# A cross-attention block: the up-projection by one level of Strassen's product

## The reference, cut to what matters

```
q = layer_norm(query, ln1_g, ln1_b)
qh = (q @ wq + bq); kh = (context @ wk + bk); vh = (context @ wv + bv)    # split into 16 heads
scores = einsum(qh, kh) / sqrt(32), causal over positions
x = query + (softmax(scores) applied to vh) @ wo + bo
h = layer_norm(x, ln2_g, ln2_b)
return x + gelu(h @ w1 + b1) @ w2 + b2          # exact GELU; w1 is 512 x 2048, w2 is 2048 x 512
```

## Time and profile before

| | us |
|---|---|
| runs (two) | 1866.86 and 1867.20, median 1867.03 |
| span of the profiled execution | 1864.5 |
| span of slots 0 and 1 | 253.8 |
| one steady slot | 108.9 |
| slot 16 | 86.5 |
| TensorE, VectorE, ScalarE, POOL busy | 1799.3, 1247.9, 640.5, 443.8 |

### The profile page before, as it was taken

How to read it: one execution, slowest core, us unless ns; L and a number is a source line. 1 busy time by engine, 2 the same in 40 slices (tenths; PEclk the granted TensorE clock), 3 DMA queues, 4 the chain that set the end, 5 groups by cost and what they waited for, 6 DMA issues and landing times.

```text
span 1864.5 us, 26584 instructions
## 1 busy us (share of the span) xinstructions
PE 1799.3 (97%) x10213; PEld 819.6 (44%) x10213; DVE 1247.9 (67%) x1930; ACT 640.5 (34%) x799; POOL 443.8 (24%) x376
## 2 busy tenths in 40 slices
PE   6678899999999999999999999999999999999999
PEld 3233344444444444444444444444444444444444
DVE  6767757667675767757676676757677576866622
ACT  5654424242232424223242422324242232424211
POOL 2523114131320314122141313203141221413200
PEclk8878999999999999999999999999999999999999
DMA  8230232314123241412323131332413133231200
GB/s 288 54 105 12 46 91 46 91 23 79 35 60 77 46 91 23 78 36 57 80 46 91 19 81 38 57 80 46 91 21 77 40 57 79 46 91 19 50 23 23
DMA packets 287738, 116.27 MB, mean 62 GB/s; under 512 B 262616, under 2 KB 264192, under 8 KB 287616
## 3 DMA queue, kind: packets, MB, share of 16 engines
q1 hardware_dynamic: 287616, 114.61, 27.4%
HBM read 31.22 MB, written 16.78 MB: 26 GB/s over the span
## 4 chain that ended last, share of the span: by engine, by line
PE 90%; DVE 5%; POOL 1%; ACT 1%; DMA 1%; issue 1%; SPq 0%; DVEq 0%; ACTq 0%
PE ff_ps L1141 34%; PE ff_ps L1384 34%; PE at_ps L1141 18%; PE at_ps L1298 2%; PE at_ps L1318 1%; DVE w_all L829 1%; POOL arena L560 1%; DVE arena L829 0%; DVE xhat L818 0%; DMA arena<-in_L_xattn_wk 0%; PE ff_ps L1213 0%; DVE arena L1114 0%; DVE arena L1061 0%; PE at_ps L1213 0%; DVE smax L1059 0%
## 5 line engine op out<-in xcount | busy, mean ns | idle before, releaser
L1141 PE MATMUL ff_ps<-arena,w_all 128*128 128x512 f16 x3072 | 701.8, 381 | 2.3 <-DVE arena L829 2.3
L1384 PE MATMUL ff_ps<-w_all,arena 128*128 128x512 f16 x3072 | 698.0, 379 | 0.9 <-DVE arena L829 0.9
L1141 PEld LDWEIGHTS ff_ps<-arena,w_all 128*128 128x128 f16 x3072 | 300.4, 98 | 371.7 <-issue 15.6
L1384 PEld LDWEIGHTS ff_ps<-w_all,arena 128*128 128x128 f16 x3072 | 294.4, 98 | 358.6 <-issue 6.4
L753 ACT ACTIVATE arena<-ff_ps,b1p,scales 128x512 f32<-128x512 f32 x256 | 198.5, 775 | 634.6 <-PE ff_ps L1141 634.3
L1114 DVE TENSOR_SCALAR arena<-arena,scales 128x512 f16<-128x512 f32 x256 | 150.1, 586 | 215.6 <-ACT arena L753 215.5
L829 DVE SCALAR_TENSOR_TENSOR arena<-arena,scales 128x512 f16<-128x512 f32 x256 | 239.2, 934 | 9.1
L511 POOL TENSOR_TENSOR rstd<-ve,minus_half 128x1 f32<-128x1 f32 x128 | 85.6, 669 | 561.1 <-DVE ve L801 561.1
L555 POOL TENSOR_TENSOR x_sb<-x_sb,bo_row 128x512 f32<-128x512 f32 x64 | 92.6, 1477 | 359.8 <-PE at_ps L1298 350.5
L687 ACT ACTIVATE norm_hl<-xhat 128x512 f16<-128x512 f32 x120 | 73.9, 628 | 287.6 <-DVE xhat L818 287.6
L560 POOL TENSOR_TENSOR arena<-arena,rsum 128x1024 f32<-128x1024 f32 x64 | 124.8, 1971 | 176.1 <-DVE rsum L1087 176.1
(11 more groups left out here) (154 smaller groups left out, 1377.3 us busy)
## 6 DMA issues: line engine op xcount, KB each, us to landing
...
```

The lines of the kernel that those rows point to most:

```text
L1141: last = nc.tensor.matmul(out_ap, s, m, start=(i == 0), stop=(i == n - 1))
L1384: last = nc.tensor.matmul(ff2_ps[:, t, :], pair[:, s, rows], m[:, j], start=(j == 0 and i == 0), stop=(j == NJ - 1 and i == 2))
```

## The change

FF1 is done in pairs of groups. For pair q the 256 hidden rows are two blocks of 128, the 512 pieces of the contraction two halves of 256, and the 512 tokens two halves of 256 columns. One level of Strassen's product in Winograd's form makes the four result quarters C11, C12, C21, C22 from seven block products instead of eight. The block sums of the weights (S1 to S4) are made once, when W1 is converted; those of the activations (T1 to T4) once per chunk, by `block_sums_of` (step K) on VectorE, so the second norm leaves seven blocks instead of four, each with its two halves (`blocks_low` and ScalarE's step D). The sums U, V and the quarters C are made on VectorE from the products in PSUM, the first product being copied to SBUF by ScalarE first. GELU then reads SBUF; its high half moves from VectorE to ScalarE.

To make room, `hT` has one buffer of seven blocks instead of two of four, keys and values of all batches lie in DRAM and are loaded per batch by ten DMAs, and the first norm's steps A and C of the next chunk move from the end of a slot to groups 1 and 2 of the next (`PLAN_NORM`, step a and c). The second norm's transposes become two of 128 x 2048, two of 128 x 1024 and two of 128 x 512.

```diff
-    25: [("O", 0), ("O", 1), ("G", 0), ("O", 2), ("G", 1), ("D", 0), ("O", 3), ("G", 2), ("D", 1),
-         ("G", 3), ("D", 2), ("D", 3)],
-    27: [("N", 0), ("N", 1), ("N", 2), ("N", 3)],
-    29: [("A", 0), ("A", 1), ("C", 0), ("A", 2)], 30: [("C", 1), ("A", 3), ("C", 2)], 31: [("C", 3)],
+    25: [("O", 0), ("O", 1), ("G", 0), ("O", 2), ("G", 1), ("K", 0), ("O", 3)],
+    26: [("D", 0), ("G", 2), ("G", 3), ("K", 1)], 27: [("N", 0), ("D", 1), ("N", 1)],
+    28: [("N", 2), ("N", 3)],
...
+PLAN_NORM = {
+    2: [("a", 0), ("a", 1), ("c", 0)], 3: [("a", 2), ("c", 1)], 4: [("a", 3), ("c", 2)], 5: [("c", 3)],
+}
...
+            def move_blocks(n, blocks, done):
+
+                sp.sem_inc(moves_begun, 1)
+                sp.dma_start_transpose(hT[:, blocks, :, :, n * P:(n + 1) * P].rearrange("p b a k n -> p (b a k) n"),
+                                       norm_blocks[n][:, blocks].rearrange("p b a n -> p (b a n)")).then_inc(done[n], 16)
...
+                    for n in range(2):
+                        sp.wait_ge(blocks_lo, 2 * c + (n + 1))
+                        sp.sem_inc(moves_begun, 1)
+                        wait(sp, first_p26, NPAIRS * c)
+                        move_blocks(n, slice(B11, T2 + 1), h_first)
+                    for n in range(2):
+                        wait(sp, second_p4, NPAIRS * c)
+                        for blocks in (slice(T1, T4 + 1), slice(B22, B22 + 1)):
+                            move_blocks(n, blocks, h_second)
...
-                        nc.scalar.activation(gelu_full[g % 2], ff1_ps[:, g % 2, :], ACT.Gelu,
-                                             bias=b1p[:, g:g + 1], scale=col(C1)).then_inc(g_full, 1)
+                    if ff and g < NJ and g % 2 == 0:
+                        q = g // 2
+                        act.wait_ge(first_p17, NPAIRS * c + (q + 1 - NPAIRS))
+                        nc.scalar.activation(quarters[:, COPY], ff1_ps[:, 0, 0:HF], ACT.Copy).then_inc(p1_moved, 1)
+                    elif ff and g < NJ:
+                        q = g // 2
+                        for j, done in ((2 * q, c12_set), (2 * q + 1, c21_set)):
+                            half = ff_in[:, j % 2 * CHUNK:(j % 2 + 1) * CHUNK]
+                            act.wait_ge(done, NPAIRS * c + (q + 1 - NPAIRS))
+                            nc.scalar.activation(half, half, ACT.Gelu, bias=b1p[:, j:j + 1], scale=col(C1)
+                                                 ).then_inc(g_full, 1)
+                            act.wait_ge(g_full, NJ * c + (j + 1 - NJ))
+                            nc.scalar.activation(g_pair[j % NG][:, 0, :], half, ACT.Copy, scale=col(SG)
+                                                 ).then_inc(g_hi, 1)
...
+            def block_sums_of(c, n):
...
+                nc.vector.tensor_tensor(t3_t1, y1.to_broadcast([P, 2, HF]), norm_f32[:, 1:3], ALU.subtract
+                                        ).then_inc(block_sums, 1)
+                dve.wait_ge(block_sums, begun + 1)
+                nc.vector.tensor_tensor(t2, y2, t1, ALU.subtract).then_inc(block_sums, 1)
+                dve.wait_ge(block_sums, begun + 2)
+                nc.vector.tensor_tensor(t4, x2, t2, ALU.subtract).then_inc(block_sums, 1)
...
+                    if ff and g < NJ and g % 2 == 0:
+
+
+                        dve.wait_ge(first_p26, NPAIRS * c + (q + 1 - NPAIRS))
+                        dve.wait_ge(p1_moved, NPAIRS * c + (q + 1 - NPAIRS))
+                        wait(dve, g_lo, NJ * c + (2 * q - NJ))
+                        nc.vector.tensor_tensor(quarters[:, C11:U + 1:4], ff1_ps[:, 1, :].rearrange("p (b n) -> p b n", b=2),
+                                                quarters[:, COPY:COPY + 1].to_broadcast([P, 2, HF]), ALU.add
+                                                ).then_inc(u_set, 1)
+                        dve.wait_ge(u_set, NPAIRS * c + (q + 1 - NPAIRS))
+                        nc.vector.tensor_tensor(quarters[:, V], ff1_ps[:, 0, HF:CHUNK], quarters[:, U], ALU.add
+                                                ).then_inc(v_set, 1)
+                    elif ff and g < NJ:
+
+
+                        dve.wait_ge(second_p53, NPAIRS * c + (q + 1 - NPAIRS))
+                        dve.wait_ge(v_set, NPAIRS * c + (q + 1 - NPAIRS))
+                        nc.vector.tensor_tensor(quarters[:, C12:C22 + 1:2],
+                                                ff1_ps[:, 0, 0:HF].unsqueeze(1).to_broadcast([P, 2, HF]),
+                                                quarters[:, U:V + 1], ALU.add).then_inc(c22_set, 1)
+                        dve.wait_ge(second_p4, NPAIRS * c + (q + 1 - NPAIRS))
+                        dve.wait_ge(c22_set, NPAIRS * c + (q + 1 - NPAIRS))
+                        nc.vector.tensor_tensor(quarters[:, C12], ff1_ps[:, 0, HF:CHUNK], quarters[:, C12], ALU.add
+                                                ).then_inc(c12_set, 1)
+                        nc.vector.tensor_tensor(quarters[:, C21], ff1_ps[:, 1, 0:HF], quarters[:, V], ALU.add
+                                                ).then_inc(c21_set, 1)
...
+                def product(q, bank, half, block, factor):
+
+
+                    weights = w1_combos[q // 2][:, q % 2]
+                    for k in range(2):
+                        for i, (s, m) in enumerate(((0, 0), (0, 1), (1, 0))):
+                            last = nc.tensor.matmul(ff1_ps[:, bank, half * HF:(half + 1) * HF],
+                                                    weights[:, s, block, k], hT[:, factor, m, k],
+                                                    start=k == 0 and i == 0, stop=k == 1 and i == 2)
+                    return last
+
+                def first_products(q):
...
+                    wait(pe, c21_set, NPAIRS * c + (q - NPAIRS))
+                    product(q, 0, 0, A11, B11)
+                    product(q, 0, 1, S3, T3).then_inc(first_p17, 1)
+                    product(q, 1, 0, A12, B21)
+                    product(q, 1, 1, S2, T2).then_inc(first_p26, 1)
+
+                def second_products(q):
...
+                    pe.wait_ge(v_set, NPAIRS * c + (q + 1 - NPAIRS))
+                    product(q, 0, 0, S1, T1)
+                    product(q, 0, 1, S4, B22).then_inc(second_p53, 1)
+                    product(q, 1, 0, A22, T4).then_inc(second_p4, 1)
...
-                        triple(ff1_ps[:, g % 2, :], [((w1_hi[:, k, cut], w1_lo[:, k, cut]), (old[:, 0, k], old[:, 1, k]))
-                                                     for k in range(KT)]).then_inc(ff1_done, 1)
+                        if g % 2 == 0:
+                            first_products(g // 2)
+                        else:
+                            second_products(g // 2)
```

More of the change, by code:

```diff
@@ L52 @@
 GROUPS = NJ + LAG
+NPAIRS = NJ // 2
+HF = CHUNK // 2
+NB = 7
+A11, A12, A22, S1, S2, S3, S4 = range(NB)
+B22, B11, B21, T3, T2, T1, T4 = range(NB)
 PLAN = {
@@ L338, in cross_attention_block @@
         conv_w1, conv_w2 = {}, {}
+        W1_STEPS = (A11, A12, S1, A22, S2, S3, S4)
         def convert_w1(n):
-            conv_w1[n] = convert_pieces(w1_raw[n], lambda k: gs2[:, k:k + 1], w1_pairs[:, n, 0], w1_pairs[:, n, 1])
+            src = {A11: w1_blocks[n][:, 0, 0], A12: w1_blocks[n][:, 1, 0], A22: w1_blocks[n][:, 1, 1],
+                   S3: w1_blocks[n][:, 0, 1]}
+            for b in W1_STEPS:
+                hi, lo = (w1_combos[n][:, :, a, b] for a in range(2))
+                conversions.append((src.get(b, w1_sum[:, :, :, :]), None, hi, lo))
+            conv_w1[n] = len(conversions)
         def convert_w2(n):
@@ L466, in slot @@
                     if first:
-                        move_values(0, slice(0, 2))
+                        store_keys()
+                        first_values()
+                    else:
+                        sp.wait_ge(o_ps, 4 * c)
+                        sp.sem_inc(moves_begun, 1)
+                        for t in range(TT):
+                            move_norm(c, t)
                     for t in range(TT):
@@ L740, in _, with slot @@
             magnitudes(W_O, 2)
-            def slot(c, par, attn, ff, batch):
+            def slot(c, par, attn, ff, batch, after):
                 first = isinstance(c, int) and c == 0
```

393 lines of the change are left out of this document (213 added, 180 removed), and 4 rows, old and new, of the table PLAN_FIRST.

## The result

The change takes 2302.4 us (median of 2 runs, 2302.2 to 2302.6) where the kernel before takes 1867.0: a ratio of 1.233, with a 95% interval of 1.228 to 1.239. The profiled execution spans 2300.6 us with a mean granted clock of 0.904. The prediction of 2278 us, 2110 to 2450, slower, held.

What follows compares the result with a forecast made beforehand. TensorE, streaming without a gap, was taken as the bound. Per slot 104.1 + 26.4 of stops + 5 of clock = 135.5, 26.6 more; 1864.5 + 14 x 26.6 + 11 + 27 = 2275 span, hence 2278 us, range 2110 to 2450.

Steps and rivals of the forecast that it cites:

- Price of a matmul: On TensorE, a 256-column FF1 matmul takes 109 ns, between 107.9 and 119; 4.8 us saved per slot.
- Groups 0 to 3: Slot's front: TensorE stops 1.4, 1.1 and, at pair 1's wait for V, 4.9 us; no wait for Q's transposes.
- Groups 7 to 9: TensorE stops 0.9 us for C21 of pair 3 and 4.7 us for V of pair 4.
- Groups 9 and 10: TensorE stops 2.5 us for U and V, behind GELUs, probability halves and low halves.
- Groups 13 to 15: Slot's end: TensorE stops 0.4 us for C21 of pair 6, then 10.5 us for V of the next pair.
- clock: Behind three or four long stops per slot TensorE runs at a lower clock, costing 5 us per slot.
- Edges: First and last slots against before: slot 0 +11 us, slot 1 +27, slot 16 0.
- one sign of being wrong: Wrong if each slot's longest wait is below 4 us, TensorE waits for a transpose, or matmuls cost 200 ns.
- the cover holds: Rival: VectorE runs far enough ahead that TensorE's stops vanish; 1815 us, chance 0.03.
- half the stops: Rival: TensorE's stops are half as long, some durations being overestimated and the clock staying up; 2007 us, chance 0.07.
- an unhidden weight load: Rival: TensorE's weight load is not hidden under 256 columns, 206 ns per matmul; about 2450 to 2600 us, chance 0.03.
- a clock low for most of the slot: Rival: clock at its lower level for much of the slot, or POOL slows the sums; above 2480 us, chance 0.04.

Runs made afterwards that it cites:

- the three orders together: Changed kernel with VectorE's and ScalarE's queued work reordered around pair 7, in groups 7 to 11 and at the slot's front: 2017.7 us, ratio 1.080.

## Why the prediction held, point by point

- **Price of a matmul**, 109 ns: 109 measured, both in the changed kernel and alone.
- **VectorE's and ScalarE's durations**: 0.43, 2.0, 1.7, 0.41 predicted; 0.425 (L1228), 2.03, 1.69, 0.37 measured; VectorE 86.6 us per slot for "some 90". One reading was wrong: the low half of 1.63 us in the earlier trace rows does not stand beside POOL's normalisation, which runs from 624.46 to 628.22, but beside POOL's additions to `x_sb` (L555, from 607.22 to 612.85). Nothing in the sum hung on it.
- **Groups 0 to 3**: 1.4 + 1.1 + 4.9 predicted, 1.43 + 0.99 + 4.85 measured (2.35 for the first in every other slot). Transposes for Q: no wait, as predicted.
- **Groups 7 to 9**: 0.9 + 4.7 predicted, 0.30 + 4.25 measured.
- **Groups 9 and 10**: 2.5 predicted, 0 to 0.69 measured. The step that failed: the walk let TensorE run at full clock behind the stop at pair 4. It ran at the low one, came later, and found VectorE done. With the clock kept up the stop is 2.26.
- **Groups 13 to 15**: 0.4 + 10.5 predicted, 0.31 + 10.56 measured.
- **Sum of stops** 26.4 predicted, 23.1 and 25.3 measured in the two slots above; **clock** 5 predicted, 7.5 and 6.1 measured. In part the two errors are one: a slow TensorE turns waiting into working. The 1.4 us of draining ahead of the stops had no term. A slot came to 136.6 for 135.5; that it is this close is in part luck, since the errors have opposite signs.
- **Edges**: slot 0 +12.4 us for +11 (its end waits 12.47 us for transposes), slot 1 166.9 us against 132.9, +34 for +27, slot 16 +1.8 for 0. These 10 us and 14 x 1.1 are the 25 by which the span of 2275 was short. By its letter one sign of being wrong came: TensorE does wait for transposes, 12.47 us once at slot 0's end and 0.28 to 0.45 us per slot at step V, too little to touch the mechanism.
- **The rivals.** That the cover holds, half the stops, an unhidden weight load and a clock low for most of the slot are each out by the rows above; that POOL slows the sums is out too, since U and V take 0.69 and 0.42 us throughout the run. The rule on rotating PSUM banks, in the Trainium skill's "Perfetto Trace Analysis", section "Optimizing Tensor Performance", pointed the right way: what the runs add is that a pair that fills both banks loses far less, 2018 us in place of 2302, by the order of the other queues alone.

No version beat 1867. What order could give at most is an estimate: 104.1 us in slots 2 to 15, with the first two slots and the last as measured after the change (300.2 and 88.2 us), is a span of about 1846; with those of the three orders together (283.8 and 86.6 us) it is about 1828, 2% under the kernel before. No run shows that a slot without stops can be had. Nor does a run separate the cost of the chain of sums from that of making room for it (one buffer for `hT`, the first norm moved to a slot's front).
